# Gate and up weights of an expert in two transfers, registers ahead of the waits, and a new order on SyncE's queue

## The chip, the cores and the metric

The kernel runs on one core of one Trainium2 chip. The metric is the device time of one execution in microseconds. The core's engines run side by side and wait for each other by semaphores: TensorE (PE) for matmuls, VectorE (DVE), ScalarE (ACT) and GpSimd (POOL) for elementwise work, and SyncE (SP), which here issues nearly all transfers (DMA). GpSimd issues the transfers with computed addresses.

## The reference, cut to what matters

```python
x = L0_attn_x                       # 1 x 4096 x 256
xn = _layernorm(x)
x = x + _L0_attn_ref(xn, ...) + _L0_ffn_ref(xn, ...)

def _L0_ffn_ref(x, gate_w, gate_b, up_w, up_b, gp_w, gp_b, down_w, down_b):
    # E = 8 experts, K = 2 for each row, F = 816 hidden columns
    scores = softmax(xf @ gate_w.T + gate_b)
    top_w, top_idx = lax.top_k(scores, K)        # weights normalised to 1
    # for every expert, added up with the row's weight w (0 where not chosen):
    h = silu((xf @ gw.T + gb) * (xf @ uw.T + ub))
    acc + w[:, None] * (h @ dw.T + db)
```

The attention part (windows of 64, layer norm, a dense network with 1024 hidden columns) comes first in the kernel. The change doesn't touch it.

## The kernel before, in words

**Two stages.** The first (to about 500 us) is attention and the dense network. It also sorts the 8192 pairs of a row and an expert by expert and writes the rows in that order to `xs_dram`. The second works through 39 **blocks** of these rows: blocks 0 to 31 have 256 rows (NF = 32), blocks 32 to 38 (NS = 7) have 128, for what is left over of the experts. Each block belongs to one expert.

**The weights of a block.** One record of an expert holds the gate and up weights for 128 partitions x 3296 numbers (GUW), in 7 chunks (FCH): six of 512 numbers (GUC) and a last one of 224. `raw_gu` has two buffers, for even and odd blocks (p = b % 2). Down weights (`raw_dw`), rows (`xr`) and biases (`bias`) have two buffers each as well. A load of weights or biases is conditional: `blk_e` holds the block's expert and a flag that is 1 where it differs from that of the block two before (the same buffer). Where it is 0 the DMA moves nothing. Both are read into registers of SyncE by `value_load`.

**Two parts for each weight.** Matmuls are made in parts: a high part, rounded to fp32r, and a low part, the remainder. Three matmuls (lines 1556 to 1558) make one product. Of the gate and up weights VectorE makes the high part of chunks 0 to 3 (`gu_high`, line 1400) and ScalarE that of chunks 4 to 6 (GA = 3, line 988); VectorE makes all low parts (`gu_low`, line 1407), and each adds 1 to the semaphore `gu_split`. Down weights: high part on ScalarE (line 995), low part of the first 4 chunks (DV) on VectorE (line 1427), of the last 3 on GpSimd (line 741).

**Who does what in the body of block b.** VectorE: for each of the 7 chunks, the product of gate and up (line 1438, the last in 1441); behind the first four of them the low part of chunks 0 to 3 of block b+1; behind the second, the low down weights of block b-1; behind the third, the weighing of block b-2's output (line 1456); at the end the high part of chunks 0 to 3 of block b+2, and then the low part of chunks 4 to 6 of block b+1. ScalarE: bias of the gate, silu, and the high part of the hidden values; at the end chunks 4 to 6 of block b+1 and the down weights of block b. GpSimd: low part of the hidden values (line 751), between the first three the low down weights of block b-1; then `keep_meta(b)` and `use_meta(b-1)` (line 734 copies the target rows `dest` and waits until the scatter of block b-3 has landed), four more low parts, and the scatter of block b-2 (line 763), a DMA that adds 128 rows of the output for each tile: two for 256 rows, one for 128. TensorE: gate and up of block b, the transposes of block b+1's rows in the middle, then down of block b-1.

**SyncE's order.** The queue waits at each step until the buffer is free:

```python
def load_block(b, p):
    load_gu(b, p)            # waits gu_split >= (b-1)*FCH: all of block b-2 split
    load_dw(b - 1, 1 - p)    # waits dw_split, dw_split_pool: block b-3's
    load_rows_of(b, p)       # waits ct_full, y_kept: block b-2's rows used
    load_bias(b, p)          # waits z_ready >= (b-1)*FCH: block b-2 done
```

`settle` adds 1 to a semaphore that nobody waits for.

Of the kernel before, what the change touches and what calls it, by code (L numbers as in the profile page):

```python
# [9 lines left out]
ds = bass.ds  # L10
# [7 lines left out]
E, F = 8, 816  # L18
# [11 lines left out]
NF = 2 * S // BT  # L30
NS = (2 * S + E * (P - 1)) // P - 2 * NF
NB = NF + NS
SLOTS = NF * BT + NS * P
REC = D + 2
FCH = 7
FR = F - (FCH - 1) * P
GRW = WIN + FR
GUC = 2 * KC * P
GUW = (FCH - 1) * GUC + KC * GRW
# [3 lines left out]
GA = 3  # L43
# [101 lines left out]
def program(nc, x, wq, wk, wv, wo, w1, w2, gate, rows, cols, gu_rec, dw_rec, bi_rec, const, out):  # L145
# [3 lines left out]
    with ExitStack() as ctx:  # L149
        def sems(names):  # L150
            return [ctx.enter_context(nc.semaphore(n)) for n in names.split()]
# [17 lines left out]
        blk_e = tile("blk_e", (1, 2 * NB), I32)  # L169
# [108 lines left out]
            "bo_ready xb_ready ln6 ln_stats ln_sd ln_rstd scaled x2_ready x2_half x2_summed")  # L278
        gelu_hi, gelu_split = sems("gelu_hi gelu_split")
        gu_loaded, dw_loaded, bi_loaded, xr_loaded = (sems(f"{n}_0 {n}_1") for n in ("gu_loaded", "dw_loaded", "bi_loaded", "xr_loaded"))  # L280
        gu_hi, gu_hi_act, gu_split, dw_hi, dw_split, dw_split_pool = sems("gu_hi gu_hi_act gu_split dw_hi dw_split dw_split_pool")
        silu_warm, last_split = sems("silu_warm last_split")
        ct_full, ct_hi, ct_split = sems("ct_full ct_hi ct_split")
# [62 lines left out]
        def settle(eng):  # L346

            eng.sem_inc(passed[eng.engine])

        def through(b, p, n):  # L350

            return (b - p) * (n // 2) + n
# [35 lines left out]
        def _(sp):  # L388
# [71 lines left out]
                fill(n)  # L460
            sp.wait_ge(pads_filled, 16)

            def load_record(dst, records, b, loaded):

                e = sp.value_load(blk_e[0:1, ds(b, 1)], min_val=0, max_val=E - 1)
                new = sp.value_load(blk_e[0:1, ds(b + NB, 1)], min_val=0, max_val=1)
                sp.dma_start(dst, records[ds(e, 1)].rearrange("o p w -> p (o w)"), cond=new).then_inc(loaded, 16)

            def load_gu(b, p, wait=True):
                if wait:  # L470
                    sp.wait_ge(gu_split, (b - 1) * FCH)
                settle(sp)
                load_record(raw_gu[:, p], gu_rec, b, gu_loaded[p])

            def load_rows_of(b, p, wait=True):
                if wait:
                    sp.wait_ge(ct_full, b - 1)
                    settle(sp)
                    sp.wait_ge(y_kept, (b - 1) * 2)
                    settle(sp)  # L480
                if tiles_of(b) == 2:
                    sp.dma_start(xr[:, p], xs_dram[ds(b * BT, BT), :].rearrange("(t p) c -> p t c", p=P)).then_inc(xr_loaded[p], 16)
                else:
                    sp.dma_start(xr[:, p, 0], xs_dram[ds((b + NF) * P, P), :]).then_inc(xr_loaded[p], 16)

            def load_dw(b, p, wait=True):
                if wait:
                    sp.wait_ge(dw_split, (b - 1) * DV)
                    settle(sp)
                    sp.wait_ge(dw_split_pool, (b - 1) * (FCH - DV))  # L490
                settle(sp)
                e = sp.value_load(blk_e[0:1, ds(b, 1)], min_val=0, max_val=E - 1)
                new = sp.value_load(blk_e[0:1, ds(b + NB, 1)], min_val=0, max_val=1)
                whole, tail = slice(0, DWW - D), slice(DWW - D, DWW)
                for at, of, cs in ((slice(0, P), slice(0, P), whole), (slice(0, WIN), slice(0, WIN), tail), (slice(WIN, P), slice(0, WIN), tail)):
                    sp.dma_start(raw_dw[at, p, cs], dw_rec[ds(e, 1), of, cs].rearrange("o p w -> p (o w)"), cond=new).then_inc(dw_loaded[p], 16)

            def load_bias(b, p, wait=True):
                if wait:
                    sp.wait_ge(z_ready, (b - 1) * FCH)  # L500
                settle(sp)
                load_record(bias[:, p], bi_rec, b, bi_loaded[p])
            def turn(at):
                b, n = m_use("Y3", at)
                sp.wait_ge(m_free[b], n + 1)
# [18 lines left out]
            sp.wait_ge(t_full[b], n)  # L524
            sp.wait_ge(slots_ready, 1)
            for b in range(2):
                load_gu(b, b, False)
            turn(CLOSING)

            b, n = m_use("O3", CLOSING)  # L530
# [11 lines left out]
            load_bias(0, 0, False)  # L542
            load_bias(1, 1, False)
            load_dw(1, 1, False)
            load_gu(2, 0)
            wait_dense_done(sp)
            store_last()
            load_rows_of(2, 0)
            load_bias(2, 0)
            def load_block(b, p):  # L550
                load_gu(b, p)
                load_dw(b - 1, 1 - p)
                load_rows_of(b, p)
                load_bias(b, p)
            with sp.Fori(0, (NF - 4) // 2) as i:
                load_block(i * 2 + 3, 1)
                load_block(i * 2 + 4, 0)
            for b in range(NF - 1, NB):
                load_block(b, b % 2)
            load_dw(NB - 1, (NB - 1) % 2)  # L560


# [235 lines left out]
        def _(act):  # L798
# [183 lines left out]

            def gu_high(b, p, c):
                if c == FCH - GA:
                    act.wait_ge(gu_loaded[p], through(b, p, 16))
                    if not isinstance(b, int) or b >= 2:
                        act.wait_ge(gu_full, (b - 1) * FCH)
                nc.scalar.activation(gu_s[p][:, 0, gu_cols(c)], raw_gu[:, p, gu_cols(c)], ACT.Copy).then_inc(gu_hi_act, 1)  # L988
# [975 lines left out]
```

## Time and profile before

| what | value |
|---|---|
| median of 3 runs | 1083.82 us (1083.06 to 1084.24) |
| the profiled execution | 1083.94 us |
| its span, first to last instruction | 1081.2 us |
| mean granted TensorE clock | 0.976 |
| TensorE busy | 1021.6 us (94% of the span) |
| VectorE, ScalarE, GpSimd busy | 844.6, 816.4, 735.0 us |
| DMA of SyncE's queue | 86.83 MB |

All engine times and rows come from the profiled execution. It is one run, and the median is what a change is measured by. The busy shares are means over two stages of different kind. TensorE's matmuls are pipelined, so it counts as busy also where each one takes longer because the granted clock is low.

### The profile page before, as it was taken

What the parts mean: (1) busy time and instruction counts of PE and PEld (TensorE: products, weight loads), DVE (VectorE), ACT (ScalarE), POOL (GpSimd) and SP (SyncE); (2) the same over time, 40 slices, a digit from 0 to 9 for tenths busy, and PEclk for the clock granted to TensorE, in tenths of its full rate; (3) what the DMA queues carried; (4) which work ended last, traced back from release to release, by engine and by line L of the source; (5) the groups of instructions that cost most, each with busy time, mean ns of one, the idle gap of its engine ahead of it and who ended that gap; (6) DMA issues with size and microseconds to landing.
All of it is one profiled execution on the core that took longest, in us unless ns stands there. A gap on an engine that the chain in (4) does not pass through costs nothing.

```text
span 1081.2 us, 28579 instructions
## 1 busy us (share of the span) xinstructions
PE 1021.6 (94%) x8622; PEld 944.6 (87%) x8622; DVE 844.6 (78%) x1962; ACT 816.4 (76%) x1983; POOL 735.0 (68%) x1038
## 2 busy tenths in 40 slices
PE   4897988999999999989999999999999999999996
PEld 3675767888888888879999999999999999999996
DVE  6568787767676767667889988988898899987773
ACT  7766756687878787867888888888888788886674
POOL 4705237275757575623688998888898888887774
PEclk9999998999999999999999999999999999999688
DMA  9980010021212111415421222246324532366641
GB/s 305 324 262 1 26 64 18 25 79 44 73 49 73 49 49 49 179 42 160 152 68 30 33 35 39 39 124 200 73 30 101 136 73 35 96 204 205 209 147 42
DMA packets 62395, 106.49 MB, mean 98 GB/s; under 512 B 8961, under 2 KB 51457, under 8 KB 60161
## 3 DMA queue, kind: packets, MB, share of 16 engines
q1 hardware_dynamic: 48496, 86.83, 24.9%
q0 software_dynamic: 13840, 18.96, 9.4%
q8 instruction: 28, 0.46, 0.2%
q14 instruction: 31, 0.25, 0.1%
HBM read 128.55 MB, written 35.59 MB: 152 GB/s over the span
## 4 chain that ended last, share of the span: by engine, by line
PE 42%; POOL 24%; issue 15%; DVE 8%; DMA 5%; ACT 5%; POOLq 1%; SPq 0%; DVEq 0%; ACTq 0%
POOL ht L751 14%; PE bank L1556 9%; PE bank L1558 8%; PE bank L1557 8%; POOL dw_s L741 5%; PE bank L1657 4%; DMA out_dram<-ys,dest 4%; POOL out_dram L763 3%; PE bank L1683 3%; PE bank L1647 3%; PE bank L1692 2%; DVE h_l L1285 1%; ACT pt L857 1%; PE bank L1703 1%; ACT sm L852 1%
## 5 line engine op out<-in xcount | busy, mean ns | idle before, releaser
L1556 PE MATMUL bank<-xt_h,gu_s 128*128 128x256 f32 (+3 forms) x1014 | 291.2, 287 | 1.9 <-DVE hf L1438 1.5
L1557 PE MATMUL bank<-xt_l,gu_s 128*128 128x256 f32 (+3 forms) x1014 | 289.2, 285 | 0.0
L1558 PE MATMUL bank<-xt_h,gu_s 128*128 128x256 f32 (+3 forms) x1014 | 288.5, 285 | 0.0
L751 POOL TENSOR_TENSOR ht<-hf,ht 128x256 fp32r<-128x256 f32 (+3 forms) x266 | 230.5, 878 | 39.4 <-ACT ht L981 29.0
L1407 DVE TENSOR_TENSOR gu_s<-raw_gu,gu_s 128x512 fp32r<-128x512 f32 (+1 forms) x273 | 198.1, 747 | 2.1 <-ACT gu_s L988 1.8
L1556 PEld LDWEIGHTS bank<-xt_h,gu_s 128*128 128x128 f32 (+1 forms) x1014 | 195.8, 193 | 2.4 <-DVE gu_s L1407 1.6
L1558 PEld LDWEIGHTS bank<-xt_h,gu_s 128*128 128x128 f32 (+1 forms) x1014 | 195.9, 193 | 0.0
L1557 PEld LDWEIGHTS bank<-xt_l,gu_s 128*128 128x128 f32 (+1 forms) x1014 | 195.4, 193 | 0.0
L969 ACT ACTIVATE gs<-bank,bias 128x256 f32<-128x256 f32 (+1 forms) x234 | 105.4, 452 | 81.7 <-PE bank L1558 75.9
L763 POOL DMA_INDIRECT out_dram<-ys,dest x71 | 120.3, 1694 | 54.1 <-POOL ht L751 30.7
L852 ACT ACTIVATE sm<-sm,least 128x256 f32<-128x256 f32 x256 | 127.0, 501 | 26.5 <-DVE least L1227 26.4
L1438 DVE SCALAR_TENSOR_TENSOR hf<-bank,bias,gs 128x256 f32<-128x256 f32 (+1 forms) x234 | 106.7, 456 | 41.3 <-ACT gs L969 20.1
L1556 PE MATMUL bank<-dw_s,ht 128*128 128x256 f32 x426 | 122.5, 288 | 2.3 <-DVE ht L1422 1.3
L1557 PE MATMUL bank<-dw_s,ht 128*128 128x256 f32 x426 | 121.8, 286 | 0.0
L1558 PE MATMUL bank<-dw_s,ht 128*128 128x256 f32 x426 | 121.7, 286 | 0.0
L977 ACT ACTIVATE hf<-hf 128x256 f32<-128x256 f32 (+3 forms) x273 | 107.4, 393 | 18.9 <-DVE hf L1438 15.1
L981 ACT ACTIVATE ht<-hf 128x256 fp32r<-128x256 f32 (+3 forms) x273 | 109.0, 399 | 10.9
L741 POOL TENSOR_TENSOR dw_s<-raw_dw,dw_s 128x256 fp32r<-128x256 f32 x114 | 106.0, 930 | 0.1
L1400 DVE CAST gu_s<-raw_gu 128x512 fp32r<-128x512 f32 x156 | 97.1, 680 | 6.9 <-DMA raw_gu<-in_gu_dram 5.9
L679 POOL DMA_INDIRECT xs_dram<-stage,sidx x64 | 63.8, 997 | 52.5 <-POOL sidx L676 48.4
L1227 DVE CUSTOM_DVE_ANT_0 sm<-bank,masks 128x256 f32<-128x256 f32 x256 | 91.0, 418 | 1.5 <-PE bank L1647 1.5
L1285 DVE TENSOR_TENSOR h_l<-h,h_h 128x512 fp32r<-128x512 f32 x64 | 61.2, 962 | 32.4 <-ACT h_h L877 31.3
(222 smaller groups left out, 2617.0 us busy)
## 6 DMA issues: line engine op xcount, KB each, us to landing
raw_gu<-in_gu_dram SPq DMA_DIRECT2D x39, 1648.0 KB
raw_dw<-in_dw_dram SPq DMA_DIRECT2D x39, 768.0 KB
xr<-xs_dram SPq DMA_DIRECT2D x32, 258.0 KB
xs_dram<-zrec SPq DMA_DIRECT2D x5, 1548.0 KB, 15.3
raw_dw<-in_dw_dram SPq DMA_DIRECT2D x78, 64.0 KB
xwin<-xt_dram SPq DMA_DIRECT2D x7, 640.0 KB, 4.4
xt_dram<-xt SPq DMA_DIRECT2D x8, 512.0 KB, 5.3
xres<-in_x_dram SPq DMA_DIRECT2D x8, 512.0 KB, 3.5
```

Source lines behind the costliest of these rows:

```text
L741: nc.gpsimd.tensor_tensor(dw_s[p][:, 1, cs], raw_dw[:, p, cs], dw_s[p][:, 0, cs].bitcast(F32), ALU.subtract).then_inc(dw_split_pool, 1)
L751: nc.gpsimd.tensor_tensor(low, hf[0:m, ring(c), 0:n], ht[0:m, p, 0, c, 0:n].bitcast(F32), ALU.subtract).then_inc(h_split, 1)
L763: nc.gpsimd.indirect_dma_start(out, bass.IndirectOffsetOnAxis(index, 0), ys[:, p, t, :], None, bounds_check=S - 1, oob_is_err=False, compu ...
L852: nc.scalar.activation(sm[:, j % 2, h, :], sm[:, j % 2, h, :], ACT.Exp, bias=least[:, j % 2, c, r:r + 1], scale=-1.0, accum_out=total[:, j ...
L969: nc.scalar.activation(gs[:, ring(c), 0:n], bank[ring(c)][:, 0:n], ACT.Identity, bias=bias[:, p, c:c + 1]).then_inc(gs_ready, 1)
L977: nc.scalar.activation(hf[0:m, ring(c), 0:n], hf[0:m, ring(c), 0:n], ACT.Silu).then_inc(hf_ready, 1)
L981: nc.scalar.activation(ht[0:m, p, 0, c, 0:n], hf[0:m, ring(c), 0:n], ACT.Copy).then_inc(hhi_ready, 1)
L1407: nc.vector.tensor_tensor(gu_s[p][:, 1, gu_cols(c)], raw_gu[:, p, gu_cols(c)], gu_s[p][:, 0, gu_cols(c)].bitcast(F32), ALU.subtract).then_ ...
L1438: nc.vector.scalar_tensor_tensor(hf[:, ring(c), 0:m], bank[ring(c)][:, BT:BT + m], bias[:, p, FCH + c:FCH + c + 1], gs[:, ring(c), 0:m], A ...
L1556: nc.tensor.matmul(dst, lhs[0], rhs[0], start=start, stop=False)
L1557: nc.tensor.matmul(dst, lhs[0], rhs[1], start=False, stop=False)
L1558: return nc.tensor.matmul(dst, lhs[1], rhs[0], start=False, stop=stop)
```

## The change

The record of gate and up weights is loaded by two DMAs in place of one: a **front** of chunks 0 to 3 (2048 of 3296 numbers for each partition) and a **rest** of chunks 4 to 6. The front waits only until chunks 0 to 3 of block b-2 are split, and keeps the semaphore `gu_loaded`; VectorE reads the front alone. The rest waits until all of block b-2 is split and has a new semaphore, `gu_rest_loaded`, for which ScalarE waits ahead of chunk 4. All loads read their registers (`record_of`) ahead of the wait on the buffer and not behind it. The order in SyncE's queue is a new one, in which each load stands where its buffer comes free.

```diff
+            gu_front, gu_rest = slice(0, (FCH - GA) * GUC), slice((FCH - GA) * GUC, GUW)
+
+            def load_gu_front(b, p, wait=True):
+                e, new = record_of(b)
+                if wait:
+                    sp.wait_ge(gu_split, (b - 2) * FCH + (FCH - GA))
+                    settle(sp)
+                sp.dma_start(raw_gu[:, p, gu_front], gu_rec[ds(e, 1), :, gu_front].rearrange("o p w -> p (o w)"), cond=new).then_inc(gu_loaded[p], 16)
+
+            def load_gu_rest(b, p, wait=True):
+                e, new = record_of(b)
                 if wait:
                     sp.wait_ge(gu_split, (b - 1) * FCH)
-                settle(sp)
-                load_record(raw_gu[:, p], gu_rec, b, gu_loaded[p])
+                    settle(sp)
+                sp.dma_start(raw_gu[:, p, gu_rest], gu_rec[ds(e, 1), :, gu_rest].rearrange("o p w -> p (o w)"), cond=new).then_inc(gu_rest_loaded[p], 16)
...
             load_rows_of(2, 0)
+            load_gu_front(3, 1)
+            load_gu_rest(3, 1)
             load_bias(2, 0)
+
             def load_block(b, p):
-                load_gu(b, p)
-                load_dw(b - 1, 1 - p)
-                load_rows_of(b, p)
-                load_bias(b, p)
+                load_gu_front(b, p)
+                load_dw(b - 2, p)
+                load_rows_of(b - 1, 1 - p)
+                load_gu_rest(b, p)
+                load_bias(b - 1, 1 - p)
             with sp.Fori(0, (NF - 4) // 2) as i:
-                load_block(i * 2 + 3, 1)
-                load_block(i * 2 + 4, 0)
-            for b in range(NF - 1, NB):
+                load_block(i * 2 + 4, 0)
+                load_block(i * 2 + 5, 1)
+            for b in range(NF, NB):
                 load_block(b, b % 2)
+            load_dw(NB - 2, NB % 2)
+            load_rows_of(NB - 1, (NB - 1) % 2)
+            load_bias(NB - 1, (NB - 1) % 2)
             load_dw(NB - 1, (NB - 1) % 2)
...
             def gu_high(b, p, c):
                 if c == FCH - GA:
-                    act.wait_ge(gu_loaded[p], through(b, p, 16))
+                    act.wait_ge(gu_rest_loaded[p], through(b, p, 16))
```

SyncE's queue before, among the blocks of 128 rows: the load of one block's gate and up weights and the start of the down load (`TENSOR_LOAD` with the `ISA` row behind it is one `value_load`; in brackets the semaphores that an instruction waits for).

```order
L465 TENSOR_LOAD blk_e [waits gu_split]
L465 ISA x2
L466 TENSOR_LOAD blk_e
L466 ISA x2
L467 ISA
L467 DMA raw_gu<-in_gu_dram 128x3296
L492 TENSOR_LOAD blk_e [waits dw_split,dw_split_pool]
```

The wait stands on the first register load, so both register loads and the DMA come behind it.

The same queue of the changed kernel, the front of a block and the down load behind it:

```order
L467 TENSOR_LOAD blk_e
L467 ISA x2
L477 ISA [waits gu_split]
L477 DMA raw_gu<-in_gu_dram 128x2048
L466 TENSOR_LOAD blk_e
L466 ISA x2
L467 TENSOR_LOAD blk_e
L467 ISA x2
L506 ISA [waits dw_split,dw_split_pool]
L506 DMA raw_dw<-in_dw_dram 128x1536
```

The wait now stands behind the register loads, and the front's DMA ahead of the down weights. And the rest, between the rows and the biases:

```order
L495 DMA xr<-xs_dram 128x258 [waits ct_full,y_kept]
L466 TENSOR_LOAD blk_e
L466 ISA x2
L467 TENSOR_LOAD blk_e
L467 ISA x2
L484 ISA [waits gu_split]
L484 DMA raw_gu<-in_gu_dram 128x1248
```

The rest stands where the whole record's wait (all of block b-2 split) is met; the front has moved ahead of the down load and the rows.

## Rows read from the trace of the kernel before

**Rows 1.** The page: its first line, and the granted clock in 40 slices.
```profile
span 1081.2 us, 28579 instructions
...
PEclk9999998999999999999999999999999999999688
```

**Rows 2.** Windows, one per VectorE body 31 to 37: busy us (instructions), clock, DMA.
```profile
958.98:974.42 15.44, 15.18 (x130) 14.97 (x128) 13.30 (x22) 11.72 (x28) 12.92 (x18) 1.00 0.64 192
974.42:987.77 13.35, 13.35 (x120) 13.35 (x119) 10.58 (x23) 9.81 (x27) 10.50 (x16) 1.00 0.78 227
987.77:1002.24 14.47, 13.05 (x102) 12.65 (x102) 10.86 (x23) 9.61 (x27) 11.78 (x17) 0.90 0.59 169
1002.24:1019.54 17.30, 17.30 (x97) 17.30 (x96) 10.69 (x21) 9.52 (x27) 11.30 (x17) 0.59 0.63 200
1019.54:1031.79 12.25, 12.25 (x112) 12.25 (x111) 10.99 (x22) 9.71 (x28) 9.34 (x16) 1.00 0.62 211
1031.79:1045.10 13.31, 12.33 (x110) 12.19 (x109) 10.21 (x21) 9.68 (x28) 10.48 (x16) 1.00 0.73 232
1045.10:1059.56 14.46, 13.96 (x82) 13.99 (x83) 9.28 (x19) 9.26 (x26) 10.67 (x17) 0.65 0.24 71
```

**Rows 3.** The waits between 940 and 1081 us: total, times, longest.
```profile
POOL dest L734 <- DMA out_dram<-ys,dest: 9.3, 5, 2.7
...
DVE gu_s L1400 <- DMA raw_gu<-in_gu_dram: 4.9, 3, 2.5
```

**Rows 4.** The chain that ended last, 940 to 1081 us: start, us, what.
```profile
975.84 8.56 DMA out_dram<-ys,dest
```

**Rows 5.** GpSimd's timeline, 935 to 1081 us.
```profile
984.55 0.26 POOL L734 COPY dest<-kept 128x2 uint32<-128x2 uint32 x1 [2.30 <-DMA out_dram<-ys,dest]
...
989.85 2.31 POOL L763 DMA_INDIRECT out_dram<-ys,dest  x1 [1.73 <-issue]
...
997.18 0.72 POOL L741 TENSOR_TENSOR dw_s<-raw_dw,dw_s 128x256 fp32r<-128x256 f32 x1
```

**Rows 6.** TensorE's timeline, 985 to 1010 and 1040 to 1056 us.
```profile
996.85 0.39 PE L1556 MATMUL bank<-dw_s,ht 128*128 128x256 f32 x1 [0.93 <-POOL dw_s L741]
...
1000.18 0.41 PE L1558 MATMUL bank<-xt_h,gu_s 128*128 128x128 f32 x1
...
1045.60 0.30 PE L1556 MATMUL bank<-xt_h,gu_s 128*128 128x128 f32 x1 [1.48 <-DVE hf L1438]
...
1047.35 0.42 PE L1557 MATMUL bank<-xt_l,gu_s 128*128 128x128 f32 x1
```

**Rows 7.** VectorE's timeline, 935 to 1081 us.
```profile
965.32 0.74 DVE L1407 TENSOR_TENSOR gu_s<-raw_gu,gu_s 128x512 fp32r<-128x512 f32 x1
...
984.00 1.44 DVE L1400 CAST gu_s<-raw_gu 128x512 fp32r<-128x512 f32 x4 [1.85 <-DMA raw_gu<-in_gu_dram]
...
1041.97 1.60 DVE L1400 CAST gu_s<-raw_gu 128x512 fp32r<-128x512 f32 x4 [2.55 <-DMA raw_gu<-in_gu_dram]
```

**Rows 8.** SyncE's timeline, 940 to 1081 us (start, us, DMA issue).
```profile
970.23 2.37 SPq L496 DMA_DIRECT2D raw_dw<-in_dw_dram  x3
...
976.61 0.33 SPq L467 DMA_DIRECT2D raw_gu<-in_gu_dram  x1
...
1053.49 1.75 SPq L496 DMA_DIRECT2D raw_dw<-in_dw_dram  x3
```

**Rows 9.** The down load's first register load (L492): ns min/median/max, first and last start.
```profile
L492 SPq TENSOR_LOAD <-blk_e x39: 262/268/281, 496.7 to 1052.1; - x39
```

**Rows 10.** GpSimd's scatters (L763), issue to landing: 550 to 700, then 940 to 1060 us.
```profile
L763 POOL DMA_INDIRECT out_dram<-ys,dest x22: 1544/1590/1949, 549.3 to 696.8; - x22
...
DMA to landing us min/median/max: 3.7/3.8/4.1
...
DMA to landing us min/median/max: 4.1/6.0/7.5
```

**Rows 11.** ScalarE's timeline, 1055 to 1070 us.
```profile
1061.31 1.78 ACT L995 ACTIVATE dw_s<-raw_dw 128x1024 fp32r<-128x1024 f32 x2
```

More of the change, by code:

```diff
@@ L280, in program @@
         gu_loaded, dw_loaded, bi_loaded, xr_loaded = (sems(f"{n}_0 {n}_1") for n in ("gu_loaded", "dw_loaded", "bi_loaded", "xr_loaded"))
+        gu_rest_loaded = sems("gu_rest_loaded_0 gu_rest_loaded_1")
         gu_hi, gu_hi_act, gu_split, dw_hi, dw_split, dw_split_pool = sems("gu_hi gu_hi_act gu_split dw_hi dw_split dw_split_pool")
@@ L461, in _, with record_of @@
             sp.wait_ge(pads_filled, 16)
-            def load_record(dst, records, b, loaded):
+            def record_of(b):
                 e = sp.value_load(blk_e[0:1, ds(b, 1)], min_val=0, max_val=E - 1)
                 new = sp.value_load(blk_e[0:1, ds(b + NB, 1)], min_val=0, max_val=1)
-                sp.dma_start(dst, records[ds(e, 1)].rearrange("o p w -> p (o w)"), cond=new).then_inc(loaded, 16)
-            def load_gu(b, p, wait=True):
+                return e, new
+            gu_front, gu_rest = slice(0, (FCH - GA) * GUC), slice((FCH - GA) * GUC, GUW)
[7 more added lines that the diff above has]
+                e, new = record_of(b)
                 if wait:
                     sp.wait_ge(gu_split, (b - 1) * FCH)
-                settle(sp)
-                load_record(raw_gu[:, p], gu_rec, b, gu_loaded[p])
+                    settle(sp)
+                sp.dma_start(raw_gu[:, p, gu_rest], gu_rec[ds(e, 1), :, gu_rest].rearrange("o p w -> p (o w)"), cond=new).then_inc(gu_rest_loaded[p], 16)
             def load_rows_of(b, p, wait=True):
@@ L486, in load_dw @@
             def load_dw(b, p, wait=True):
+                e, new = record_of(b)
                 if wait:
@@ L491, in load_dw @@
                 settle(sp)
-                e = sp.value_load(blk_e[0:1, ds(b, 1)], min_val=0, max_val=E - 1)
-                new = sp.value_load(blk_e[0:1, ds(b + NB, 1)], min_val=0, max_val=1)
                 whole, tail = slice(0, DWW - D), slice(DWW - D, DWW)
@@ L498, in load_bias @@
             def load_bias(b, p, wait=True):
+                e, new = record_of(b)
                 if wait:
@@ L501, in load_bias @@
                 settle(sp)
-                load_record(bias[:, p], bi_rec, b, bi_loaded[p])
+                sp.dma_start(bias[:, p], bi_rec[ds(e, 1)].rearrange("o p w -> p (o w)"), cond=new).then_inc(bi_loaded[p], 16)
             def turn(at):
@@ L526, in _ @@
             for b in range(2):
-                load_gu(b, b, False)
+                load_gu_front(b, b, False)
+                load_gu_rest(b, b, False)
             turn(CLOSING)
@@ L544, in _ @@
             load_dw(1, 1, False)
-            load_gu(2, 0)
+            load_gu_front(2, 0)
+            load_gu_rest(2, 0)
             wait_dense_done(sp)
```

## The prediction

> **What bounds the kernel now.** Read the clock first. The granted TensorE clock stands at 9 tenths or more in nearly every slice, and falls near the end, to 6 and 8 tenths [rows 1]. Then cut the end of the span at the starts of VectorE's bodies, 31 to 38 (a body is VectorE's work for one block; bodies 32 to 38 are the seven blocks of 128 rows) [rows 2]. TensorE is busy without a gap in body 32, but the next bodies cost 14.47, 17.30, 12.25, 13.31 and 14.46 us for the same 128-row work. Two things differ between them. TensorE idles 1.42 us in body 33, 0.98 in body 36 and 0.50 in body 37 (window less busy time), 2.9 us in all. And the granted clock is 0.90, 0.59 and 0.65 in bodies 33, 34 and 37, 1.00 in 35 and 36. What the missing clock is worth: 0.10 x 14.47 + 0.41 x 17.30 + 0.35 x 14.46 = 13.6 us. Idle time and clock together are 16.5 us. The 400 us before are different: body 31 loses 0.26 us [rows 2], and the clock is at 9 tenths or more in all slices that cover them [rows 1]. So the question is what makes the two short TensorE gaps behind which the clock falls.
>
> The timelines answer it. First fall: the scatter of an older block is issued at 975.84 and lands 8.56 us later [rows 4]; GpSimd waits 2.30 us for it, then issues its own next scatter slowly (2.31 us, where 1.59 is the median of the calm stretch) and ends the low half of the down weights only at 997.90 [rows 5, 10]. TensorE, in the down projection, asks for the first of them at 995.92 and waits 0.93 us [rows 6], and soon again for the last. A gate/up matmul that starts at 1000.18 takes 0.41 us, which is the 1.2 GHz level; the same form at the 2.4 GHz level took 0.30 at 1045.60 [rows 6]. Second fall: VectorE waits 2.55 us at 1041.97 for the gate/up weights [rows 7]; TensorE starves 1.48 us until 1045.60, and at 1047.35 it runs 0.42 us a matmul [rows 6]. So TensorE did the same before each fall: it had stood for about a microsecond and a half. Both gaps come from loads. The scatter is slow only where weights are loaded: 3.8 us median (3.7 to 4.1) between 550 and 700 us, where experts don't change, 6.0 (4.1 to 7.5) in the last stage [rows 10]. Waits on these two transfers are 9.3 us on GpSimd and 4.9 us on VectorE [rows 3].
>
> **The change part by part.**
>
> Earlier front. The whole record of block 34, 128 x 3296 x 4 B = 1.69 MB, is issued at 976.61 [rows 8] and VectorE gets it at 984.00, after 7.4 us (228 GB/s) and a wait of 1.85 us [rows 7]; VectorE was ready 5.5 us after the issue. The front is 128 x 2048 x 4 = 1.05 MB and waits only for chunk 3 of block 32, which VectorE ends at 966.06 (965.32 + 0.74) [rows 7]. So it leaves some 10 us sooner and is smaller: at 228 GB/s it takes 4.6 us, with 16 us to its use. VectorE's 4.9 us of waits for it go to nothing. The rest (0.64 MB, 2.8 us at the same rate) leaves about where the whole left before, and ScalarE reads it only at the end of body 33 (the window to 1002.24), over 20 us later: hidden.
>
> A calmer time for the scatter. GpSimd's two-tile scatter leaves about when the 1.69 MB left (975.84 against 976.61). Now 0.64 MB leaves there, and the 1.05 MB is in by 971 (966.1 + 4.6), ahead of it. The scatter's landing should go from 8.6 us towards the 3.8 to 4.1 of the calm stretch [rows 4, 10]. The wait of 2.30 us is gone once it takes under 6.4 us (982.25, where GpSimd begins to wait, less 975.84) [rows 5]. With that alone the down weights of 997.90 are ready at 995.6; TensorE asked for the first of the three at 995.92. The margin is 0.3 us by this term alone, and 1.0 us if the slow scatter issue (2.31 against 1.59 us) goes as well.
>
> Registers ahead of the wait. From the first register load at 1052.1 to the down load's DMA at 1053.49 are 1.4 us, which stood behind the wait [rows 8, 9]. Now they stand ahead of it, if SyncE has time. It has four pairs in place of three: 4 x 1.4 = 5.6 us, the down load's issues 2.37, four other issues at about 0.33, together 9.3 us in a body of 11.5 [rows 8]. It fits, with 2 us to spare. Nothing on the path waits for those 1.4 us except perhaps the last down load, below.
>
> One more DMA a block. 39 more issues at 0.33 us on SyncE, all in its slack; per block the bytes are the same. The trace has no split record, so its price is bounded: nothing below, and above 0.3 us of issue in each of seven loading blocks, 2.3 us, if SyncE were on the path. I take nothing, since 16 us lie ahead of the front's use. From the row, 7.4 us for the whole, 2 us more would still end inside those 16 us. The Trainium skill (DMA: Bandwidth & Descriptors) speaks against the split: its section "Bandwidth" asks for transfers of at least 1 MiB, and the fit in "Anatomy of one DMA", 2.0 us and the bytes over 436 GB/s, gives 5.9 us for the whole and 4.4 + 3.5 = 7.9 us for the parts. By that rule seven blocks would cost 14 us more of transfer, and 1085 if nothing hid them; no run here shows such a price.
>
> Order of the others. Down weights, rows and biases of a block are released by the same events as before and only stand behind the front instead of ahead of the whole record. The down load, issued at 970.23, now has up to 1.05 MB ahead of it (4.6 us) and its own 0.92 MB (4.0 us); its use is a body and more away: hidden. The exception is block 38, used already after its first chunk. There the issue at 1053.49 has 7.8 us to its use at 1061.31 [rows 8, 11]. Body 37 shrinks by 3 us, the registers give 1.4 back, which leaves 6.2 us for 4.0. I charge 0.5 us for what may still be late, 0 to 1.5 as bounds. At the start of the stage, block 2's bias now stands behind block 3's rest; it is used a body later: nothing.
>
> The sum. What does a clean 128-row body take? Bodies 35 and 36 ran at clock 1.00; without VectorE's 2.55 us they take (12.25 + 13.31 - 2.55) / 2 = 11.5 us [rows 2, 7]. TensorE alone would allow 10.9: a block has 78 matmuls for gate/up, 20 for down and 2 transposes, at 12.25 us for 112. Bodies 33 to 37 took 71.8 us. Clean they take 5 x 11.5 = 57.5, and 1.0 more in body 33, where GpSimd alone was busy 11.78 us with its two-tile scatters: 58.5 us. Gain 13.3. Body 31 gives its 0.26, body 32 nothing (TensorE was full there, so the 1.85 us of VectorE were hidden). Less the 0.5: 13.0 us. The profiled execution took 1083.94 us (its span 1081.2), the median of the runs shown is 1083.82; 1083.9 - 13.0 = 1070.9.
>
> **The rivals.**
>
> A, forecast: both gaps go and the clock stays. For it: each fall has one gap ahead of it, each gap one late transfer, and bodies 35 and 36 show 128-row blocks at full clock. Floor: TensorE's 10.9 us a body, 54.5 for five, 17.3 less than 71.8, so with body 31 1066.4. Chance 0.52, own range 1066.5 to 1075.
>
> B, one fall stays or comes elsewhere. For it: the margin of 0.3 us of GpSimd's term above; GpSimd and VectorE are both nearly full in these bodies (11.8 and 11.0 us) [rows 2]. Price: the first fall costs 7.1 + 1.4 = 8.5 us of clock, the second 5.1. So 1076 to 1079.5. Chance 0.20.
>
> C, the loads are early but TensorE gaps all the same, because GpSimd's own work paces it; both falls stay. Then only what VectorE's waits cost TensorE comes back, at most the 1.5 us at 1045.60, with 1 us of body 31 and the scatters. 1081 to 1084, half of it within 0.2%. Chance 0.16. That the change is hidden altogether belongs here.
>
> D, slower: the front is the new thing in the scatter's way. In body 33 the second scatter left some 4.7 us after the body began (989.85 + 2.31 + 0.3 of gap, less 987.77) [rows 2, 5]; the front of block 36 leaves at about 5.5 us into it (chunk 3). If the scatter lands slower than about 6 us there, GpSimd waits in bodies where it did not, and TensorE gaps a third time. It decides where the landing passes the 7.5 us seen at worst [rows 10] by about 1 us. Price: a gap of 1.4 and a fall of 8.5 us on top of the two that stay, less the 4.4 us of VectorE's two long waits: about 1089. The same sign comes if SyncE's 9.3 us grow past 11.5, so that it falls behind by a body. Against it: 0.64 MB lands in 2.8 us, before the front leaves. Chance 0.12.
>
> **How the numbers follow.** A measurement of this kernel tells about 0.2%, 2.2 us, from no change. Faster: A, B and under half of C, 0.79. Within 0.2%: 0.09. Slower: 0.12. The time is A's, 1070.9. The range goes from TensorE's floor, 1066.5, through B to the start of C, 1082.
>
> **What would show it right or wrong.** VectorE's idle time for raw_gu near zero. GpSimd's wait at the copy of dest under 4 us in all, and the scatter's landing median in the last stage at 4 to 5 us. TensorE without a gap over 0.5 us between 985 us and its last block, the clock 1.00 through bodies 33 to 37, and these bodies 11 to 12.5 us long. The span before 940 us unchanged within 1 us. In the changed kernel the fronts must be issued in the middle of a body and the rests at its end. I am wrong if the waits go and the clock still falls (then the falls had another cause, B or C), or if GpSimd's waits grow (D).

## The result, and the profile after

The changed kernel took 1073.0 us (median of 4 runs, 1071.94 to 1074.55), the kernel before 1083.44 us beside it (4 runs). The ratio is 0.9907, 95% interval 0.9889 to 0.9926: faster by 10.4 us (1%), where 13.0 were forecast. The profiled execution of the changed kernel took 1071.94 us, its span 1070.1, at a mean granted clock of 0.985 (before 0.976).

The windows of VectorE's bodies 31 to 37 and of the end (from body 38's start to the last instruction), with the columns of [rows 2]:

```profile
958.30:972.50 14.20, 14.20 (x123) 14.20 (x122) 13.07 (x22) 11.67 (x27) 12.66 (x17) 1.00 0.72 207
972.50:985.95 13.45, 13.45 (x121) 13.45 (x120) 11.42 (x22) 9.53 (x27) 11.17 (x17) 1.00 0.78 228
985.95:998.19 12.24, 12.24 (x112) 12.24 (x111) 10.88 (x23) 9.49 (x28) 10.68 (x17) 1.00 0.76 223
998.19:1010.62 12.43, 11.42 (x102) 11.28 (x102) 10.59 (x22) 9.53 (x28) 10.89 (x17) 1.00 0.77 246
1010.62:1022.41 11.79, 11.43 (x102) 11.30 (x102) 10.89 (x21) 9.61 (x28) 10.21 (x16) 1.00 0.68 206
1022.41:1036.98 14.57, 13.44 (x93) 13.30 (x92) 10.79 (x22) 9.55 (x27) 11.02 (x16) 0.77 0.52 163
1036.98:1049.17 12.19, 12.19 (x112) 12.19 (x110) 9.35 (x19) 9.66 (x28) 9.15 (x15) 1.00 0.26 81
1049.17:1070.10 20.93, 10.96 (x93) 10.51 (x92) 8.90 (x19) 7.29 (x22) 8.72 (x13) 0.90 0.09 10
```

Body 31 began at 958.30, before at 958.98 [rows 2], so only 0.7 us of the gain lie ahead of it and all the rest behind it. Body 34 lost its low clock (17.30 to 12.43 us), bodies 33 and 37 took 12.24 and 12.19 in place of 14.47 and 14.46. But body 36 became longer, 14.57 after 13.31, at a clock of 0.77: one fall is left, in a body that had none.

TensorE's gaps in the same stretch (its timeline from 985 to 1044 us, the rows with idle time ahead of them):

```profile
1001.64 0.44 PE L1873 MATMUL bank<-cst,xr 128*128 128x128 f32 x2 [1.01 <-DMA xr<-xs_dram]
...
1013.40 0.44 PE L1873 MATMUL bank<-cst,xr 128*128 128x128 f32 x2 [0.36 <-DMA xr<-xs_dram]
...
1025.95 0.44 PE L1873 MATMUL bank<-cst,xr 128*128 128x128 f32 x2 [1.13 <-DMA xr<-xs_dram]
```

The gaps of before, behind GpSimd's down weights and VectorE's gate/up weights [rows 6], are gone. Three new ones stand ahead of the transposes of the next block's rows, a wait that before had no part in them. The chain that ended last has them too:

```profile
995.95 5.65 DMA xr<-xs_dram
...
1020.70 5.20 DMA xr<-xs_dram
```

SyncE's timeline shows what stands ahead of them (start, us, DMA issue):

```profile
992.11 0.33 SPq L477 DMA_DIRECT2D raw_gu<-in_gu_dram  x1
994.01 1.75 SPq L506 DMA_DIRECT2D raw_dw<-in_dw_dram  x3
995.95 0.43 SPq L495 DMA_DIRECT2D xr<-xs_dram  x1
998.38 0.34 SPq L484 DMA_DIRECT2D raw_gu<-in_gu_dram  x1
```

The rows (132 KB) are issued 3.84 us behind a front of 1.05 MB and 1.94 us behind a down load of 0.92 MB, and land 5.65 us later. Of the clock, windows of 2 us show the fall behind the last gap (busy us of PE, PEld, DVE, ACT and POOL, clock, DMA share, GB/s):

```profile
1024.00:1026.00 2.00, 0.87 (x9) 0.73 (x8) 2.00 (x4) 0.84 (x4) 2.00 (x2) 1.00 0.97 309
1026.00:1028.00 2.00, 2.00 (x19) 2.00 (x19) 2.00 (x4) 0.83 (x4) 2.00 (x4) 1.00 0.31 74
1028.00:1030.00 2.00, 2.00 (x15) 2.00 (x13) 1.16 (x4) 1.42 (x6) 2.00 (x7) 0.61 0.03 8
1030.00:1032.00 2.00, 2.00 (x11) 2.00 (x11) 1.21 (x4) 1.67 (x7) 0.99 (x3) 0.50 0.59 184
```

At 0.50, the 1.2 GHz level, TensorE does 11 matmuls in 2 us where it did 19 to 21 at 2.4 GHz. No fall came behind the gap of 1.01 us at 1001.64. GpSimd's waits for the scatter's landing:

```profile
  DMA out_dram<-ys,dest: 2.4, 1
...
DMA to landing us min/median/max: 3.5/4.8/6.5
```

That is 2.4 us once, at the end, where it was 9.3 in five [rows 3], and 4.8 us to landing where it was 6.0 [rows 10].

### The profile page after: what moved, and what is told of

Read it like the earlier page. It is cut to its first block, busy times and chain, and to the rows that moved or that the text cites. A ratio compares the mean times of both kernels' runs of the same rounds, so it can differ in the third digit from the quotient of the medians.

```text
span 1070.1 us, 29018 instructions
## 1 busy us (share of the span) xinstructions
PE 1011.5 (95%) x8622; PEld 935.4 (87%) x8622; DVE 846.5 (79%) x1962; ACT 815.0 (76%) x1983; POOL 737.1 (69%) x1038
## 4 chain that ended last, share of the span: by engine, by line
PE 40%; POOL 27%; issue 16%; DVE 9%; ACT 5%; DMA 2%; POOLq 1%; SPq 1%; DVEq 0%; ACTq 0%
POOL ht L771 14%; PE bank L1576 8%; PE bank L1578 8%; PE bank L1577 8%; POOL dw_s L761 6%; PE bank L1677 5%; POOL out_dram L783 4%; PE bank L1703 3%; PE bank L1667 3%; PE bank L1712 2%; DVE h_l L1305 1%; DMA xr<-xs_dram 1%; ACT pt L877 1%; ACT sm L872 1%; PE bank L1723 1%
## 5 line engine op out<-in xcount | busy, mean ns | idle before, releaser
L1576 PE MATMUL bank<-xt_h,gu_s 128*128 128x256 f32 (+3 forms) x1014 | 287.3, 283 | 0.4 <-DVE xt_l L1467 0.4
L1577 PE MATMUL bank<-xt_l,gu_s 128*128 128x256 f32 (+3 forms) x1014 | 285.2, 281 | 0.0
L1578 PE MATMUL bank<-xt_h,gu_s 128*128 128x256 f32 (+3 forms) x1014 | 284.5, 281 | 0.0
L1427 DVE TENSOR_TENSOR gu_s<-raw_gu,gu_s 128x512 fp32r<-128x512 f32 (+1 forms) x273 | 192.9, 728 | 1.6 <-ACT gu_s L1008 1.4
L1576 PEld LDWEIGHTS bank<-xt_h,gu_s 128*128 128x128 f32 (+1 forms) x1014 | 192.0, 189 | 0.9 <-DVE xt_l L1467 0.6
L1578 PEld LDWEIGHTS bank<-xt_h,gu_s 128*128 128x128 f32 (+1 forms) x1014 | 191.9, 189 | 0.0
L1577 PEld LDWEIGHTS bank<-xt_l,gu_s 128*128 128x128 f32 (+1 forms) x1014 | 191.4, 189 | 0.0
L783 POOL DMA_INDIRECT out_dram<-ys,dest x71 | 115.6, 1628 | 52.5 <-POOL ht L771 30.7
L761 POOL TENSOR_TENSOR dw_s<-raw_dw,dw_s 128x256 fp32r<-128x256 f32 x114 | 115.3, 1012 | 0.1
L1420 DVE CAST gu_s<-raw_gu 128x512 fp32r<-128x512 f32 x156 | 103.1, 717 | 1.1
```

The lines of the kernel that those rows point to most:

```text
L761: nc.gpsimd.tensor_tensor(dw_s[p][:, 1, cs], raw_dw[:, p, cs], dw_s[p][:, 0, cs].bitcast(F32), ALU.subtract).then_inc(dw_split_pool, 1)
L783: nc.gpsimd.indirect_dma_start(out, bass.IndirectOffsetOnAxis(index, 0), ys[:, p, t, :], None, bounds_check=S - 1, oob_is_err=False, compu ...
L1427: nc.vector.tensor_tensor(gu_s[p][:, 1, gu_cols(c)], raw_gu[:, p, gu_cols(c)], gu_s[p][:, 0, gu_cols(c)].bitcast(F32), ALU.subtract).then_ ...
L1576: nc.tensor.matmul(dst, lhs[0], rhs[0], start=start, stop=False)
L1577: nc.tensor.matmul(dst, lhs[0], rhs[1], start=False, stop=False)
L1578: return nc.tensor.matmul(dst, lhs[1], rhs[0], start=False, stop=stop)
```

## The experiments

All ratios are to the kernel before, timed beside each on the same chip. "From body 32" is the profiled execution's time from VectorE's body 32 to the last instruction: 106.8 us before (974.42 to 1081.2), 97.6 after. It is used since the first stage varies by some us between executions.

**1. The changed kernel once more**, over more executions.

> The changed kernel once more, on the chip of the three runs beside it, as their measure. In its profile the two waits on the gate/up weights are gone, but TensorE waits three times for a new one, the rows xr of the next block (1.0, 0.4 and 1.1 us), and behind the third the clock falls once. Theory 1 (each fall follows a gap that a late transfer makes): the same three waits, one fall near body 36, 1071 to 1075 us. Theory 2 (the blocks of 128 rows lower the clock by themselves, gaps or none): falls of another number and at other places than in the first profile.

Measured: 1075.91 us (1071.26 to 1083.58, 12 runs), ratio 0.9932 (0.9911 to 0.9953). Its gaps at the rows were 0.58, 1.27 and 1.30 us, with two falls, behind the last two. Its median is nearly 3 us over the first one, though the ratios' intervals overlap. So the changed kernel has no single time: its mean granted clock over the runs went from 0.975 to 0.986, where the one profile of the first result had 0.985.

**2. Rows ahead of the down load.** One swap in the changed kernel:

```diff
                 load_gu_front(b, p)
+                load_rows_of(b - 1, 1 - p)
                 load_dw(b - 2, p)
-                load_rows_of(b - 1, 1 - p)
                 load_gu_rest(b, p)
```

> The changed kernel with one edit: the rows of a block are loaded ahead of the down weights and not behind them. Theory 1: the rows land some 3 us earlier (0.92 MB fewer ahead of them), TensorE's 2.5 us of waits for them go to under 0.5 us, the clock stays at 1.00 through bodies 33 to 37, and the time is 1066 to 1069 us, 3 to 6 below the changed kernel. Theory 2: the waits go, a fall stays, 1070 to 1073.

Measured: 1068.92 us (1067.62 to 1070.14, 5 runs), ratio 0.9869 (0.9852 to 0.9886). It has the lowest median and, over its five runs, a spread of only 2.5 us (by ratio experiment 8 is level with it): every run had a clock of 0.986 to 0.988. No wait of TensorE for `xr` is left, and the largest of its gaps from 985 us to body 38 is this:

```profile
1011.45 0.30 PE L1576 MATMUL bank<-xt_h,gu_s 128*128 128x128 f32 x1 [0.37 <-DVE hf L1458]
```

```profile
998.77:1010.95 12.18, 12.18 (x110) 12.16 (x109) 11.20 (x22) 9.81 (x28) 10.64 (x17) 1.00 0.75 231
1010.95:1022.75 11.80, 11.37 (x101) 11.16 (x99) 10.89 (x21) 9.23 (x27) 10.56 (x16) 1.00 0.78 251
1022.75:1034.57 11.82, 11.60 (x103) 11.38 (x102) 10.90 (x21) 9.41 (x28) 10.25 (x16) 1.00 0.51 153
```

Clock 1.00 in each (bodies 34 to 36). 94.2 us from body 32 on. So most of what the changed kernel still lost came from the wait for the rows.

**3. The record whole again**, registers ahead and the new order kept; the gate/up load stands where the rest stood (written here as `load_gu_whole`):

```diff
             def load_block(b, p):
-                load_gu_front(b, p)
                 load_dw(b - 2, p)
                 load_rows_of(b - 1, 1 - p)
-                load_gu_rest(b, p)
+                load_gu_whole(b, p)
                 load_bias(b - 1, 1 - p)
```

> The record in one transfer again, as before, at the place of the rest: only the registers ahead of the waits are left of the change. Theory 1: VectorE's waits for the weights shrink by the 1.4 us of the register loads (4.9 to about 1.5 us in all), the scatter still lands late behind 1.69 MB, so the first fall stays and the second may go: 1077 to 1082 us. Rival (the registers were the whole gain, the split is idle): 1071 to 1075, as the changed kernel.

Measured: 1071.45 us (1069.3 to 1073.99, 6 runs), ratio 0.9897 (0.9879 to 0.9916). The rival's time came, not that of my theory: without the split the gain is all there. (Not only the registers are left, as the expectation has it: the biases also stand behind the gate/up load now. Experiments 5 and 6 take the two apart.) And the scatter was no calmer than before:

```profile
  DMA out_dram<-ys,dest: 3.7, 4
...
DMA to landing us min/median/max: 2.7/6.7/8.6
```

**4. No gate/up traffic in the last stage.** In the kernel before, each block of 128 rows loads 256 of the 3296 numbers of a partition, of other weights, and computes with what is in the buffer; the rest of its gate and up weights is left out.

```diff
+                if isinstance(b, int) and b >= NF:
+                    sp.dma_start(raw_gu[:, p, 0:D], dw_rec[0:1, :, 0:D]...).then_inc(gu_loaded[p], 16)
+                else:
+                    load_record(raw_gu[:, p], gu_rec, b, gu_loaded[p])
```

> The kernel before, but for the blocks of 128 rows the gate/up load brings only 256 of 3296 numbers for each partition; the rest of their weights is left out (they compute with what lies in the buffer). So its time shows what the loads cost in all ways. Theory 1: no waits for weights, scatters land in 4 to 5 us, no gap over 0.5 us, clock 1.00 in bodies 33 to 37: 1066 to 1070 us. Theory 2: the falls stay although nothing is late: 1078 to 1084 us.

Measured: 1073.46 us (1071.1 to 1076.94, 6 runs), ratio 0.9915 (0.9895 to 0.9934); clock 1.00, 93.9 us from body 32 on. Its body 32 began at 977.43, 3 us later than before, which is why the whole time is no lower. Body 30 was already 3.1 us late (947.63 against 944.51), ahead of what the edit changes. TensorE still waited for rows twice (0.71 and 0.35 us), and no fall followed. So some 94 us are what this stage takes without that traffic, and experiments 2 and 3 are at 94.2.

**5. Registers alone.** The kernel before, whole record and old order, only `record_of` ahead of each wait:

```diff
+                e, new = record_of(b)
                 if wait:
                     sp.wait_ge(gu_split, (b - 1) * FCH)
-                settle(sp)
-                load_record(raw_gu[:, p], gu_rec, b, gu_loaded[p])
+                    settle(sp)
+                sp.dma_start(raw_gu[:, p], gu_rec[ds(e, 1)]..., cond=new).then_inc(gu_loaded[p], 16)
```

> The kernel before with one edit: in all three loads of weights and biases the registers are read ahead of the wait. The record is whole and the order is the old one, so the biases of a block still stand ahead of the next gate/up load. Theory 1 (what counts is how early the gate/up record leaves after its wait; with registers and order together it left about 3 us earlier and all gaps were gone): here it leaves about 1.4 us earlier, VectorE's waits of 1.85 and 2.55 us shrink to 0.5 and 1.2, GpSimd's scatter is as late as before, so at least one fall is gone: 1072 to 1079 us. Rival (the order was the gain): 1081 to 1084.

Measured: 1073.06 us (1072.06 to 1074.43, 4 runs; before beside it 1085.52), ratio 0.9879 (0.9856 to 0.9903). This one edit brings as much as the whole change. The loads leave earlier: before, the whole record of block 34 was issued 2.2 us after body 32 began (976.61 against 974.42 [rows 2, 8]), here 0.3 us after it (971.90 against 971.59), and the down load ahead of it 5.5 us before that start in place of 4.2. VectorE's first wait of before is gone, but it still waited once for the gate/up weights (2.32 us, before 2.55 [rows 7], where 1.2 were expected), and behind the TensorE gap that followed came the kernel's one fall:

```profile
1025.55 0.30 PE L1557 MATMUL bank<-xt_h,gu_s 128*128 128x128 f32 x1 [2.28 <-DVE hf L1439]
```

The first fall of before was gone, though GpSimd still waited 6.9 us in five for scatters, which took 6.8 us to land (median).

**6. Order alone.** New order, whole record, registers behind the waits (the `load_block` of experiment 3, with `e, new = record_of(b)` behind each wait).

> The whole record in one transfer with the new order (down weights, rows, gate/up, biases), registers behind the wait as in the kernel before. So against the kernel before only the biases have moved behind the gate/up load. Theory 1: it leaves some 0.3 to 1.7 us earlier, where the biases held it back: 1074 to 1082 us. Rival (the registers were the gain): 1081 to 1084.

Measured: 1078.43 us (1076.33 to 1083.87, 11 runs), ratio 0.9945 (0.9926 to 0.9964). Two falls. Behind gaps of 0.68 and 0.47 us ahead of GpSimd's down weights, much like those of the first fall of before, the clock stayed. It fell at 1005.1, 1.2 us after a gap of 0.66 us that ended at 1003.88. The second fall comes in body 38, 1.5 us after this gap, and lasts 3.4 us:

```profile
1058.15 0.30 PE L1565 MATMUL bank<-xt_h,gu_s 128*128 128x128 f32 x1 [0.72 <-DVE hf L1447]
```

**7. The change with registers behind the waits**, here for the front; the other three loads are edited alike.

```diff
             def load_gu_front(b, p, wait=True):
-                e, new = record_of(b)
                 if wait:
                     sp.wait_ge(gu_split, (b - 2) * FCH + (FCH - GA))
                     settle(sp)
+                e, new = record_of(b)
```

> The changed kernel with one edit: the registers are read behind each wait again; two transfers and the order of the change stay. Theory 1: the front has 10 us to spare, so VectorE does not wait; but the rows leave later, 1.4 us at most, behind front and down weights, TensorE's waits for the rows grow to 1.5 to 2.5 us each and more falls follow: 1077 to 1086 us. Rival (the split gives what is gained): 1071 to 1076.

Measured: 1080.35 us (1077.77 to 1082.09, 6 runs), ratio 0.9946 (0.9926 to 0.9966). The waits for the rows grew, and each of the two long ones has a fall. The first fall came 0.7 us after the gap, the second began inside its gap, 0.7 us after TensorE had stopped:

```profile
1003.50 0.44 PE L1873 MATMUL bank<-cst,xr 128*128 128x128 f32 x2 [2.73 <-DMA xr<-xs_dram]
...
1032.76 0.69 PE L1873 MATMUL bank<-cst,xr 128*128 128x128 f32 x2 [1.93 <-DMA xr<-xs_dram]
```

**8. Split, but late.** The changed kernel, with the front directly ahead of the rest, where experiment 3 has the whole record:

```diff
             def load_block(b, p):
-                load_gu_front(b, p)
                 load_dw(b - 2, p)
                 load_rows_of(b - 1, 1 - p)
+                load_gu_front(b, p)
                 load_gu_rest(b, p)
```

> The record in two transfers, both issued where the whole one stood in the run with the registers ahead of the wait and the record whole; the front has no earlier wait. Against that run only one more DMA a block. If a second DMA costs its issue alone, 1071 to 1073 us and a body of 11.5 to 12 us; if it costs 2 us of transfer a block on the path, VectorE waits again and a fall comes back: 1076 to 1082.

Measured: 1070.74 us (1068.73 to 1072.7, 4 runs), ratio 0.9855 (0.9831 to 0.9878): not slower than the whole record. The Trainium skill (DMA: Bandwidth & Descriptors, "Bandwidth") asks for transfers of at least 1 MiB. The 14 us that the prediction worked out from that page (by the fit in "Anatomy of one DMA", which is of one transfer issued by GpSimd, where these are SyncE's) did not come here. The profiled execution had a fall behind gaps of 0.48 and 0.21 us, from 1002.0 on; experiment 3 had nearly the same gaps and none. TensorE's rows of this kernel, then a window behind them:

```profile
999.42 0.30 PE L1576 MATMUL bank<-xt_h,gu_s 128*128 128x128 f32 x1 [0.48 <-DVE hf L1458]
...
1001.16 0.44 PE L1873 MATMUL bank<-cst,xr 128*128 128x128 f32 x2 [0.21 <-DMA xr<-xs_dram]
```

```profile
1002.00:1004.00 2.00, 2.00 (x11) 2.00 (x11) 1.98 (x5) 0.99 (x4) 1.93 (x4) 0.50 0.95 339
```

The same of experiment 3:

```profile
1000.45 0.30 PE L1565 MATMUL bank<-xt_h,gu_s 128*128 128x128 f32 x1 [0.47 <-DVE hf L1447]
...
1002.17 0.44 PE L1862 MATMUL bank<-cst,xr 128*128 128x128 f32 x2 [0.19 <-DMA xr<-xs_dram]
```

```profile
1004.00:1006.00 2.00, 2.00 (x21) 2.00 (x20) 1.55 (x4) 1.46 (x5) 2.00 (x4) 1.00 0.98 403
```

**9. Whole record and rows first**: experiment 3 with the swap of experiment 2.

> The run with the record whole and the registers ahead of the waits, and the rows loaded ahead of the down weights: a version without the split. Theory (a body's time is TensorE's unless a late transfer makes a gap; the split is not needed): the last wait for the rows, 0.2 us, goes too, the clock stays at 1.00, 1067 to 1071 us, level with or just under the split kernel with its rows first (1068.9). Rival (the split gives something of its own): 1071 to 1075.

Measured: 1072.86 us (1069.58 to 1076.92, 6 runs), ratio 0.9901 (0.9868 to 0.9934). That is in the rival's range, and its ratio lies above experiment 2's (0.9869) with overlapping intervals: that the split gives something of its own once the rows go first is neither shown nor excluded. With the whole record the swap brings nothing that can be told. The down weights come later, and TensorE now waited for GpSimd (0.74 and 0.49 us) and for VectorE, which waited 1.6 us for gate/up weights. The longest of these gaps had no fall behind it in the profiled execution:

```profile
1024.71 0.30 PE L1565 MATMUL bank<-xt_h,gu_s 128*128 128x128 f32 x1 [1.57 <-DVE hf L1447]
```

```profile
1026.00:1028.00 2.00, 2.00 (x21) 2.00 (x20) 2.00 (x5) 0.99 (x4) 1.93 (x3) 1.00 0.80 310
```

But the mean clock over its six runs went from 0.978 to 0.989, so some of them probably had one.

**10 and 11. One gap made on purpose**, in experiment 9's kernel: the rows of block 36 wait for a chunk of block 35's gate/up matmuls, the second in one kernel, the third in the other.

```diff
+                if isinstance(b, int) and b == NF + 5:
+                    sp.wait_ge(gu_full, (b - 2) * FCH + 2)    # + 3 in the other
                 load_rows_of(b - 1, 1 - p)
```

> The whole-record version with its rows first, with one wait added: SyncE issues the rows of block 36 only when TensorE has done two chunks of block 35's gate and up, 2.7 us before it needs them. Theory of the clock (it falls behind a TensorE gap of about a microsecond, at some 8 to 10 us of half clock each): here the gap is 0 to 1 us, and mostly no fall follows: 0 to 2 us over the version without the wait.

> The same, but after three chunks, 1.35 us before TensorE needs the rows: one gap of 1.5 to 2.5 us and nothing else late. Theory of the clock: one fall behind it, so the gap and 4 to 5 us more: 5.5 to 8 us over the version without the wait. Rival (the low clock comes from the blocks of 128 rows and not from gaps): the time grows by the gap alone, 1.5 to 2.5 us.

Measured: 1078.58 us (1075.62 to 1081.06, 12 runs) and 1077.33 us (1073.98 to 1079.73, 7 runs), ratios 0.9951 (0.9933 to 0.9968) and 0.9931 (0.9906 to 0.9956). The gap that was meant did not come: at the rows it was nothing in the first and 0.49 us in the second, since the rows landed 2.1 us after their issue. Yet both took more than experiment 9 (5.7 and 4.5 us by the medians, 5.4 and 3.3 by the ratios, whose intervals touch or overlap), and both profiles have one fall: in the first 0.2 us after a gap of 0.65 us behind VectorE, in the second 0.7 us after the 0.49 us at the rows. Both expectations, 0 to 2 and 5.5 to 8 us, missed. The wait also held up what stands behind it on SyncE, the down and gate/up loads (VectorE waited 2.6 and 3.1 us for gate/up weights), so these two don't isolate anything.

**12. The same gap in the cleanest kernel**, experiment 2's, with a wait for the fourth chunk.

```diff
+                if isinstance(b, int) and b == NF + 5:
+                    sp.wait_ge(gu_full, (b - 2) * FCH + ROWS_AT)
                 load_rows_of(b - 1, 1 - p)
```

> The changed kernel with the rows ahead of the down load (1068.92 us, clock 1.00 to the end, no TensorE gap over 0.5 us in its last stage), and one thing more: the rows of block 36 are issued only when TensorE has ended chunk 4 of block 35's gate/up, which is just when it wants to transpose them. The rows landed 2.1 us after their issue in an earlier run, so this makes one TensorE gap of 2 to 2.5 us in body 35, in a kernel that has no other. Theory 1 (a gap of this length brings a fall of the clock behind it): 2 to 2.5 us of gap and 4 to 8 of clock, 1075 to 1079 us, the clock at the 1.2 GHz level for some 10 us behind the gap in the profile. Theory 2 (the gap alone doesn't do it, the falls had other causes or hang on chance): 1070.5 to 1072 us and a clock of 1.00. A spread of over 5 us between the single runs would say that it is met in some runs and not in others.

Measured: 1073.52 us (1073.23 to 1075.5, 4 runs), ratio 0.9898 (0.988 to 0.9917), 4.6 us over experiment 2. All four runs had a clock of 0.981 to 0.984, below every run of experiment 2. TensorE's rows, body 35's window, and windows of 2 us:

```profile
1010.09 0.30 PE L1578 MATMUL bank<-xt_h,gu_s 128*128 128x128 f32 x1 [0.66 <-DVE hf L1460]
...
1013.86 0.69 PE L1875 MATMUL bank<-cst,xr 128*128 128x128 f32 x2 [2.24 <-DMA xr<-xs_dram]
```

```profile
1009.59:1025.91 16.32, 13.58 (x83) 13.47 (x83) 10.88 (x22) 9.28 (x26) 11.13 (x16) 0.69 0.65 202
...
1012.00:1014.00 2.00, 0.14 (x1) 0.15 (x2) 2.00 (x4) 0.64 (x3) 2.00 (x2) 0.61 0.32 77
1014.00:1016.00 2.00, 2.00 (x11) 2.00 (x11) 1.48 (x3) 0.00 (x0) 2.00 (x4) 0.50 0.58 163
...
1022.00:1024.00 2.00, 2.00 (x17) 2.00 (x15) 2.00 (x4) 2.00 (x5) 1.04 (x2) 0.83 0.85 315
```

2.24 us of gap and 0.31 x 16.32 = 5.1 us of missing clock, of which the first 1.4 us cost nothing, since TensorE stood. Body 35 took 4.5 us more than in experiment 2 (16.32 against 11.80). From body 32 on it is 100.3 us, 6.1 more, but 1.1 of them are in body 33, ahead of the wait that was added. The medians give 4.6, the ratios (0.9898 and 0.9869) 3.1. The time, 1073.52, lies between the two forecasts (1070.5 to 1072 and 1075 to 1079): over the 2 to 2.5 us of a gap alone and under the forecast with a fall.

Two things keep this from being a clean proof. The clock fell at 1012.45, 0.8 us after TensorE had stopped and 1.4 us before it went on, so the length of 2.24 us was not what brought it. And a gap of 0.66 us (0.37 in experiment 2) had ended 2.4 us before that fall; gaps of this size have falls behind them in experiments 6 and 10. The kernel that it started from was also not free of gaps, as the expectation says: it has one of 1.44 us in body 38.

**Over all profiles**, one execution of each kernel, from body 32 to the end:

| falls in the 128-row bodies | kernels | from body 32, us |
|---|---|---|
| none | experiments 2, 3, 4, 9 | 94.2, 94.2, 93.9, 96.8 |
| one | after, 5, 8, 10, 11, 12 | 97.6, 101.0, 98.4, 100.4, 99.4, 100.3 |
| two | before, 1, 6, 7 | 106.8, 101.5, 100.1, 107.9 |

## Why the prediction came out as it did

**What bounds the kernel: held.** TensorE bounds it, the loss was idle time and the clock behind it, and all of it lay in the last stage. The floor that experiment 4 shows is 12.9 us under before; the prediction's sum was 13.0.

**"Earlier front": the wait went as forecast, but the split was not needed for it.** VectorE's waits for `raw_gu` are gone (before 4.9 us [rows 3]). So are they in experiment 3, with the whole record at the old place, issued at 973.51 us where it was 976.61 [rows 8]. To give the front the credit was the first wrong step.

**"A calmer time for the scatter": not the cause.** In the changed kernel the landing came down to 4.8 us. In experiment 3 it was 6.7, with 8.6 at most, and that kernel had no fall; in experiment 5 GpSimd still waited 6.9 us and the first fall was gone. The chain from the slow scatter to the first fall explains one execution; a calmer scatter is not what the gain needs.

**"Nothing on the path waits for those 1.4 us": this is the step that failed.** Registers ahead of the waits, which the sum took at nothing, bring 12.5 us alone (experiment 5, 1085.52 to 1073.06, ratio 0.9879), no less than the whole change. Out of experiment 3 they take some 5 us (0.9945 in experiment 6 against 0.9897), out of the change 1.5 to 4, which overlapping intervals leave vague (0.9946 in experiment 7 against 0.9932 and 0.9907). Experiments 6 and 7 say what the split is worth where registers stay behind: nothing (order alone 0.9945, order and split 0.9946). The 1.4 us come once in each load, and each load lets the next one start sooner: in experiment 5 the issues around the starts of bodies 32 and 33 are 0.3 to 1.9 us earlier, counted from these starts, than before. That transfers and the engines' shares of the weights therefore end earlier all along the stage is the likely reason; it was not isolated. The prediction priced them as SyncE's time and not as the start of every transfer. Which of the loads matters most was not tried.

**"One more DMA": nothing, as taken.** Experiment 8 is level with experiment 3.

**"Order of the others": wrong for one of them.** The sentence that down weights, rows and biases only stand behind the front was followed by a price for the down weights and one for the bias, and by none for the rows. These have only the time from TensorE's transposes of one block to those of the next, and with 2 MB ahead of them they took 5.65 us. This made the new gaps, and the one fall left: rival B, a fall that "comes elsewhere", in part. Experiment 2 gives the price: 4.1 us against the changed kernel's first median, 7.0 against that of experiment 1.

**The sum.** Bodies 33 to 37 took 63.2 us (12.24 + 12.43 + 11.79 + 14.57 + 12.19), not 58.5: a gain of 8.6 in place of 13.3. Bodies 31 and 32 together gave 1.1 and the end (from body 38's start) 0.7 us (21.64, which is 1081.2 - 1059.56, to 20.93), and the stage began 0.7 earlier. That makes the 11.1 us by which the span is shorter. The clean body of 11.5 us was sized rightly: experiment 3 has 11.53, 11.54 and 11.47 us, experiment 2 11.8. The size came out near by luck. By the prediction's own test ("I am wrong if the waits go and the clock still falls") its mechanism failed, and of its signs TensorE without a gap over 0.5 us and the clock at 1.00 in bodies 33 to 37 did not come. What came was rival B's mechanism, one fall, at a time in A's range, since this fall cost only 0.23 x 14.57 = 3.4 us where B took 5.1 or 8.5. Over more executions (experiment 1, 1075.91) the time is at the edge of B's 1076 to 1079.5.

**What stays open.** Whether a given gap brings a fall. In experiment 12 gaps of 0.66 and 2.24 us together cost 3.1 to 5.0 us, with a lower clock in all four runs. Length is no rule: gaps of 1.01 (after) and 1.57 us (experiment 9) had none, gaps of 0.66 and 0.72 us had one each (experiment 6), while 0.68 and 0.47 us just before had none, and gaps of 0.48 and 0.21 us had one in one kernel and none in another. In body 38 every profile but experiment 6's has a gap of 1.4 to 1.7 us ahead of the last down projection, and in none did the clock fall in the 2 to 3 us of work that were left. In the 128-row bodies no fall came without a gap ahead; more is not shown.

## What to carry to other kernels

Where a queue waits for a buffer, everything that doesn't need the buffer (register loads above all) belongs ahead of the wait: count the time between wait and DMA as lateness of that transfer, not as work of the queue. When a large transfer is moved forward, list for every load that it passes the time from its issue to its use; the small one with the shortest of these times is where the new wait appears, and one swap may give it back. Near the full clock, look for short TensorE gaps: where the clock fell, the price was up to six times their length (8.5 us of clock behind 1.4 us in the kernel before), and whether it fell varied from run to run. Here the version with the smallest gaps before body 38 was also among the steadiest (0.986 to 0.988 in five runs).

## What was not expected of the hardware

A fall keeps TensorE at the 1.2 GHz level for 3 to 17 us, though it is busy all or nearly all of the time: 3.4 us in body 38 of experiment 6, 0.23 x 14.57 / 0.5 = 6.7 us in body 36 of the changed kernel, 0.31 x 16.32 / 0.5 = 10.1 us in experiment 12, and (0.10 x 14.47 + 0.41 x 17.30) / 0.5 = 17 us in the first of before [rows 2]. The same kernel's mean clock differed by 1% between executions on one chip (0.975 to 0.986 in experiment 1), and its time by 12 us.

A split record with its rows first (experiment 2) gave bodies of 11.8 us, against 11.5 for the whole one (experiment 3). VectorE's high parts took 687 ns each in experiment 2 and 467 in experiment 3 (1000 to 1035 us), and its low parts of 512 columns 755 against 780. In experiment 3 GpSimd sometimes still waits for a scatter when the high parts begin; in experiment 2 it works beside them. The Trainium skill (SBUF — State Buffer, "SBUF: two separate sides") says that VectorE and GpSimd share a port pair which one instruction holds alone; the durations of the high parts agree with it, those of the low parts don't show it, and no run isolated it.
